# Two more rows of the attention weights turned by VectorE, one transfer group fewer for TensorE, and a shorter ring of rooms

## What is computed

```python
def _attention(q, k, v):
    logits = jnp.einsum('bqhd,bkhd->bhqk', q.astype(jnp.float32), k.astype(jnp.float32))
    logits = logits / jnp.sqrt(jnp.float32(q.shape[-1]))
    logits = jnp.where(mask, logits, neg)
    probs = jax.nn.softmax(logits, axis=-1).astype(dtype)
    return jnp.einsum('bhqk,bkhd->bqhd', probs, v)
...
xn = _layernorm(x, axis=-1)
x = x + _L0_attn_ref(xn, w_qkv, w_out) + _L0_ffn_ref(xn, wg, w1, b1, w2, b2)
```

## Time and profile before

| | |
|---|---|
| median of 3 runs | 2915.57 us (2914.02 to 2918.3) |
| the profiled execution, its own time | 2915.7 us |
| its span, first to last instruction | 2913.9 us |
| mean granted TensorE clock | 0.988 |
| PE busy | 2814.5 us (97%) |
| DVE busy | 2084.7 us (72%) |
| ACT busy | 1699.7 us (58%) |
| POOL busy | 1723.0 us (59%) |

### The profile page before, as it was taken

One profiled execution on the slowest core, in us unless ns is written; L12 is line 12 of the kernel. 1 busy time (PEld: TensorE's weight loads), 2 busy tenths in 40 slices (PEclk: granted clock), 3 DMA queues, 4 the chain that ended last, 5 costly groups with the idle time before them and its releaser, 6 DMA issues.

```text
span 2913.9 us, 61264 instructions
## 1 busy us (share of the span) xinstructions
PE 2814.5 (97%) x21321; PEld 2284.1 (78%) x21321; DVE 2084.7 (72%) x4448; ACT 1699.7 (58%) x3934; POOL 1723.0 (59%) x2631
## 2 busy tenths in 40 slices
PE   5599999999998999999999999999999999999998
PEld 4489999899997777777777777777777777777776
DVE  7843444344434888888888888888888888888886
ACT  3454444445454666666666666666666666666664
POOL 3032122211212777777877877777777778777774
PEclk9799999999999999999999999999999999999999
DMA  7022212221212565665665565665665556556553
GB/s 241 29 82 75 69 52 83 76 68 47 82 54 74 141 158 144 163 154 145 168 150 145 147 170 147 157 166 142 157 164 151 149 146 176 141 145 183 136 134 93
DMA packets 248774, 371.58 MB, mean 128 GB/s; under 512 B 77392, under 2 KB 177744, under 8 KB 248480
## 3 DMA queue, kind: packets, MB, share of 16 engines
q1 hardware_dynamic: 216000, 276.31, 35.3%
q0 software_dynamic: 32480, 91.44, 11.7%
HBM read 102.80 MB, written 33.55 MB: 47 GB/s over the span
## 4 chain that ended last, share of the span: by engine, by line
PE 66%; DVE 1%; SPq 1%; DMA 0%; issue 0%; ACT 0%; POOL 0%; DVEq 0%; ACTq 0%
PE O L1263 18%; PE S L1231 16%; PE W L1142 12%; PE W L1157 7%; PE W L1176 7%; PE W L1187 6%; SPq L1085 1%; DVE pr L1355 0%; PE W L1165 0%; DMA pT<-squares 0%; DVE squares L1398 0%; ACT pr L1293 0%; DMA out<-res 0%; ACT pT L1283 0%; DVE res L1381 0%
## 5 line engine op out<-in xcount | busy, mean ns | idle before, releaser
L1436 POOL TENSOR_SCALAR pr<-pr,rinv 128x512 f32<-128x512 f32 (+7 forms) x1024 | 748.4, 744 | 399.7 <-DVE rinv L1361 398.6
L1293 ACT ACTIVATE pr<-pr,negm 128x512 f32<-128x512 f32 (+7 forms) x1024 | 787.3, 774 | 285.3 <-DVE negm L1355 285.3
L1355 DVE CUSTOM_DVE_ANT_0 pr<-S,late 128x512 f32<-128x512 f32 (+7 forms) x1024 | 717.0, 751 | 112.9 <-PE S L1231 112.9
L1263 PE MATMUL O<-pT,vv 128*64 128x256 f32 (+1 forms) x5120 | 541.3, 362 | 3.1 <-DMA pT<-squares 3.1
L1398 DVE STREAM_TRANSPOSE squares<-pr 128x640 f32<-128x640 f32 x504 | 494.8, 1020 | 0.0
L1263 PEld LDWEIGHTS O<-pT,vv 128*64 128x64 f32 x5120 | 346.4, 137 | 181.8 <-issue 20.4
L832 DVE TENSOR_TENSOR hl<-h,hh 128x512 fp32r<-128x512 f32 x256 | 192.3, 751 | 315.2 <-ACT hh L793 315.0
L789 ACT ACTIVATE h<-pH,b1c 128x512 f32<-128x512 f32 x256 | 175.9, 687 | 366.0 <-PE pH L719 334.1
L1283 ACT ACTIVATE pT<-W 128x512 f32<-128x512 f32 (+3 forms) x520 | 199.6, 437 | 215.8 <-PE W L1187 215.8
L731 PE MATMUL pY<-w2h,hh 128*128 128x256 f32 x1024 | 287.7, 281 | 2.5 <-DVE hl L832 2.5
L731 PE MATMUL pY<-w2l,hh 128*128 128x256 f32 x1024 | 289.1, 282 | 0.0
(11 more groups left out here) (176 smaller groups left out, 6479.6 us busy)
## 6 DMA issues: line engine op xcount, KB each, us to landing
pT<-squares SPq DMA_DIRECT2D x756, 128.0 KB
pT<-squares SPq DMA_DIRECT2D x756, 96.0 KB, 2.8
pT<-squares POOLq DMA_DIRECT2D x252, 128.0 KB
pT<-squares POOLq DMA_DIRECT2D x252, 96.0 KB, 3.0
y<-yb SPq DMA_DIRECT2D x128, 128.0 KB, 1.7
wr<-in_L_attn_w_qkv SPq DMA_DIRECT2D x128, 128.0 KB, 2.3
x<-in_L_attn_x SPq DMA_DIRECT2D x16, 512.0 KB, 8.9
xn<-xn SPq DMA_DIRECT2D x16, 512.0 KB, 4.4
```

What stands on the lines that cost most here:

```text
L1263: ins = e.matmul(O[hs, o0 + a:o0 + GQ], vv[n // 2 % 2][:, kt, vs], turned_p, start=(kt == 0), stop=(kt == KT - 1))
L1293: e.activation(p, p, ACT.Exp, bias=negm[:, c0:c0 + 1], scale=-1.0, accum_out=rsum[:, c0:c0 + 1]).then_inc(expd.sem, 1)
L1355: e.tensor_tensor_reduce(room_of(n, i, h)[:, off:off + w], S[h][:, off:off + w], late[:, SEQ - w:], 1.0, -MASKED, ALU.add, ALU.min, negm[: ...
L1436: e.tensor_scalar(p, p, rinv[:, c0:c0 + 1], 1.0, ALU.mult, ALU.mult).then_inc(scaled.sem, 1)
```

## The change

Rows 3 and 2 are turned by DVE in squares as rows 4 to 7 are. Their squares lie next to those of rows 4 and 5 in one buffer (`squares12`), and one group of 16 transfers moves both groups 1 and 2 to `pT12`; a transfer of it is 32 x 1280 elements instead of 32 x 768. PE's pieces t30, t31, t20 and t21 and ACT's copies of them are gone. The rooms are two rounds instead of three. Row 1 and row 0 are still turned by PE, but one round earlier: t1 at step 8 instead of 13, t0 at step 12 instead of 16. Row 1 is scaled ahead of row 4. Run 0 stands at step 7 instead of 3 and run 1 at step 11 instead of 7. Several pieces move: v1 from step 4 to 2, p1 from 10 to 4, o0 and o1 to steps 9 and 10, o2 from 11 to 13. On DVE the low part of a projection and `xnl` stand ahead of the squares of their step. In the last unit only rows 6 and 7 are still turned by PE.

```diff
-    SUB, RING = 4, 3
+    SUB, RING = 4, 2
-    SCALE_ORDER = [(i, h) for rows in ROUNDS for i in (rows if 0 not in rows else rows[::-1]) for h in range(2)]
+    SCALE_ORDER = [(i, h) for rows in ROUNDS for i in (rows if 3 in rows else rows[::-1]) for h in range(2)]
...
-    SQUARED = [4, 5, 6, 7]
-    in_squares = lambda n, i: i in SQUARED and n < UNITS - 1
+    SQUARED = [(i, h) for i in (3, 2, 4, 5, 6, 7) for h in range(2)]
+    TURNED_LAST = (6, 7)
+    in_squares = lambda n, i: i > 1 and (n < UNITS - 1 or i not in TURNED_LAST)
...
-    ACT_STEP = {"v0": 2, "xn": 2, "v1": 6, "t30": 8, "t31": 8, "t20": 8, "t21": 9, "p1": 12,
-                "p0": 12, "t1": 13, "t0": 16, "p2": 17, "p3": 18}
-    DVE_STEP = {"xn": 3, "o0": 6, "o1": 10, "p1": 12, "o2": 12, "p0": 15, "p2": 19, "p3": 19, "o3": STEPS + 2}
+    ACT_STEP = {"v0": 2, "xn": 2, "v1": 4, "p1": 6, "t1": 8, "t0": 12, "p0": 13, "p2": 17, "p3": 18}
+    DVE_STEP = {"xn": 2, "p1": 6, "o0": 10, "o1": 10, "p0": 14, "o2": 15, "p2": 18, "p3": 19, "o3": STEPS}
...
-    RUN_STEP = [(1, 3), (1, 7), (1, 15)]
+    RUN_STEP = [(1, 7), (1, 11), (1, 15)]
...
-                e.wait_ge(squared.sem, squared.at(n, 4 * g - 4))
+                e.wait_ge(squared.sem, squared.at(n, 4 * g))
...
-                if x == 2 and 0 <= m < UNITS and in_squares(m, ROUNDS[q][0]):
-                    for h in range(2):
-                        square(m, ROUNDS[q][0], h)
+                if x == 2 and 0 <= m < UNITS:
+                    for i in ROUNDS[q]:
+                        if in_squares(m, i):
+                            for h in range(2):
+                                square(m, i, h)
```

More of the change, by code:

```diff
@@ L874, in attention_and_sum @@
     column = lambda n, i, h: 4 * room(n, i) + 2 * ROUNDS[ROUND_OF[i]].index(i) + h
-    SQUARED = [4, 5, 6, 7]
-    in_squares = lambda n, i: i in SQUARED and n < UNITS - 1
-    TURNS = {"t30": [(3, 0, 0, 4)], "t31": [(3, 1, 0, 4)], "t20": [(2, 0, 0, 3)], "t21": [(2, 1, 0, 3)],
-             "t1": [(1, 0, 0, 2), (1, 1, 0, 2)], "t0": [(0, 0, 0, 1), (0, 1, 0, 1)]}
-    TURNS |= {f"t{i}{h}{c}": [(i, h, c * HT, min(HT, i + 1 - c * HT))] for i in SQUARED for c in range(-(-(i + 1) // HT)) for h in range(2)}
@@ new lines, in attention_and_sum @@
+    TURNS = {"t1": [(1, 0, 0, 2), (1, 1, 0, 2)], "t0": [(0, 0, 0, 1), (0, 1, 0, 1)]}
+    TURNS |= {f"t{i}{h}{c}": [(i, h, c * HT, min(HT, i + 1 - c * HT))] for i in TURNED_LAST for c in range(-(-(i + 1) // HT)) for h in range(2)}
+    STEP_OF = {"v0": 0, "xn": 1, "v1": 2,
+               "p1": 4,
+               "t1": 8, "o0": 9, "o1": 10,
+               "t0": 12, "p0": 12, "o2": 13,
+               "p2": 16, "p3": 17, "o3": 18}
+    ACT_STEP = {"v0": 2, "xn": 2, "v1": 4, "p1": 6, "t1": 8, "t0": 12, "p0": 13, "p2": 17, "p3": 18}
@@ L899, in attention_and_sum @@
+    DVE_STEP = {"xn": 2, "p1": 6, "o0": 10, "o1": 10, "p0": 14, "o2": 15, "p2": 18, "p3": 19, "o3": STEPS}
+    BANK_OF = {"v0": 0, "xn": 2, "v1": 1,
+               "p1": 2,
+               "t1": 2, "o0": 1, "o1": 0,
+               "t0": 2, "p0": 1, "o2": 0,
+               "p2": 0, "p3": 1, "o3": 2}
+    END_STEP = {6: (UNITS, 0), 7: (UNITS, 4)}
     DVE_STEP |= {f"t6{h}{c}": 2 for h in range(2) for c in range(2)}
@@ L953, in attention_and_sum @@
         vv = two(lambda i: sb(f"vv{i}", [P, QT, VW]))
-        pT = [sb(f"pT{g}", [P, 2, 2 * g + 2, GQ]) for g in range(GROUPS)]
-        sq = {g: sb(f"squares{g}", [P, QUARTERS, 4, 2 * g + 2, BL]) for g in (2, 3)}
-        wide = {g: pT[g][:].rearrange("p h k q -> p (h k q)").rearrange("p (a x r) -> p a x r", x=4, a=QUARTERS) for g in (2, 3)}
+        BLOCK = {g: 4 * (2 * g + 2) * BL for g in (1, 2, 3)}
+        pT0, pT3 = (sb(f"pT{g}", [P, 2, 2 * g + 2, GQ]) for g in (0, 3))
+        pT12, sq12 = (sb(n, [P, QUARTERS, BLOCK[1] + BLOCK[2]]) for n in ("pT12", "squares12"))
+        sq3 = sb("squares3", [P, QUARTERS, BLOCK[3]])
+        pT = {0: pT0[:], 3: pT3[:]}
+        wide = {1: pT12[:, :, :BLOCK[1]], 2: pT12[:, :, BLOCK[1]:],
+                3: pT3[:].rearrange("p h k q -> p (h k q)").rearrange("p (a r) -> p a r", a=QUARTERS)}
+        wide = {g: w.rearrange("p a (x r) -> p a x r", x=4) for g, w in wide.items()}
+        sq = {1: sq12[:, :, :BLOCK[1]], 2: sq12[:, :, BLOCK[1]:], 3: sq3[:]}
+        sq = {g: w.rearrange("p b (x k i) -> p b x k i", x=4, i=BL) for g, w in sq.items()}
+        whole = {2: (pT12[:], sq12[:]), 3: (wide[3].rearrange("p a x r -> p a (x r)"), sq3[:])}
         pr = start.pr + [sb(f"pr{i}", [P, SEQ]) for i in range(len(start.pr), 2 * RING)]
@@ L1026, in _ @@
             def _(e):
-                for g in (2, 3):
+                for g in (1, 2, 3):
                     e.memset(sq[g][:, :, 0::2, 2 * g + 1, :], 0.0)
@@ L1032, in attention_and_sum @@
         recip = Count(sem("s_recip"), len(ROUNDS))
-        squared = Count(sem("s_squared"), 2 * len(SQUARED))
+        squared = Count(sem("s_squared"), len(SQUARED))
         placed = {2: Count(sem("s_placed2"), 16 * QUARTERS * (QUARTERS - 1)), 3: Count(sem("s_placed3"), 16 * QUARTERS * (QUARTERS - 1))}
@@ L1066, in strip @@
             to, of = slice(b * BL, (b + 1) * BL), slice(a * BL, (a + 1) * BL)
-            return wide[g][to, a].rearrange("p x r -> p (x r)"), sq[g][of, b].rearrange("p x k i -> p (x k i)")
+            placed_in, squares = whole[g]
+            return placed_in[to, a], squares[of, b]
         @block.sync
@@ L1117, in _ @@
                         refill(b, g)
-                if n < UNITS - 1:
-                    place(n, 2)
+                place(n, 2)
                 if n % 2 == 0 and n // 2 + 2 < UNITS // 2:
@@ L1237, in values @@
                 groups = RUN_GROUPS[j]
[L1238 to L1247, removed]
+                for g in groups:
+                    if in_squares(n, 2 * g):
+                        e.wait_ge(placed[max(g, 2)].sem, placed[max(g, 2)].at(n + 1, 0))
+                        e.wait_ge(pool_placed[max(g, 2)].sem, pool_placed[max(g, 2)].at(n + 1, 0))
+                    else:
+                        for m, name in [(turn_unit(n, t), t) for i in (2 * g, 2 * g + 1) for t in turns_of(i)]:
+                            if by_act(name):
+                                e.wait_ge(act.sem, act.at(m, name))
+                            else:
+                                e.wait_ge(dve.sem, dve.at(m, name))
                 if j == 0:
@@ L1348, in row_min @@
                             if in_squares(m, of):
-                                e.wait_ge(squared.sem, squared.at(m, 2 * SQUARED.index(of) + h + 1))
+                                e.wait_ge(squared.sem, squared.at(m, SQUARED.index((of, h)) + 1))
                             else:
@@ L1393, in square @@
                 g, KT = i // 2, i + 1
-                if n > 0 and i % 2 == 0 and h == 0:
-                    e.wait_ge(placed[g].sem, placed[g].at(n, 0))
-                    e.wait_ge(pool_placed[g].sem, pool_placed[g].at(n, 0))
+                if n > 0 and i in (3, 6) and h == 0:
+                    e.wait_ge(placed[max(g, 2)].sem, placed[max(g, 2)].at(n, 0))
+                    e.wait_ge(pool_placed[max(g, 2)].sem, pool_placed[max(g, 2)].at(n, 0))
                 e.wait_ge(scaled.sem, scaled.at(n, SCALE_ORDER.index((i, h)) + 1))
@@ L1518, in _ @@
                         place_rest(n - 1, 3)
-                    elif name == "place2" and n < UNITS - 1:
+                    elif name == "place2":
                         place_rest(n, 2)
```

## The result

The changed kernel takes 3130.45 us (median of 4 runs; one of them, 3422.56 at a mean granted clock of 0.748 where the others had 0.965 or 0.966, is left out of the ratio). Measured beside it, the kernel before took 2914.8 us. The ratio is 1.0738, with a 95% interval of 1.0717 to 1.0759: 7.4% slower. The prediction was 3130 us, in a range of 3045 to 3190. The profiled execution took 3129.8 us, with a span of 3128.0, 214.1 more than before.

A forecast was written before the change was run, and what follows sets the result against it. A loop through PE, DVE and POOL was to bound the unit at 33.35 us, 2.54 above before: 2915.7 + 160 = 3076 us, plus 54 for the clock = 3130. Range 3045 to 3190, 80 in 100.

The forecast's parts named there:

- The loop: Once per unit through PE, DVE and POOL: 13.63 + 6.85 + 11.48 + 1.19 + 0.20 hand-overs = 33.35 us.
- The waits for ACT: DVE waits for ACT's copies in each unit: 0.70 us ahead of `ql`, 0.82 of `xnl`, 0.91 of `klf`.
- One way out of the list: From r1's reciprocals on DVE, the loop was followed only through POOL's scaling of row 1 (1.19 us) to t1.
- Where PE waits: PE idles 4.36 us per unit: some 3.3 at t1, the rest ahead of S1 and S2.
- The clock: PE's waits lower its clock, 1.7 us per unit: nothing to 107 us in all, the middle, 54, taken.
- Two rounds of rooms at nothing: Row minima waiting for turns two rounds back cost nothing; t1 and t0 are over before r3 and r4 begin.
- The larger transfers at nothing: SP's 12 issues take 7.54 us, leaving some 6 us for the last to land before run 0; no cost.
- The last units: In the last unit 22 fewer transposes and a later run 0 about cancel, within 3 us.
- PE without gaps: Rival: row 1 is scaled before PE reaches t1; unit 28.99 us, kernel 2801; 6 in 100.
- DVE's waits for ACT: Rival: the three waits, 2.43 us together, vanish; loop 30.92 us, kernel 2923; 6 in 100.
- The squares do not hold POOL: Rival judged: new squares on DVE delay POOL's row 1 by up to 2.18 us; kernel 3267; 5 in 100.
- transfers set the unit: Sign of a wrong forecast: PE's waits at the runs for transfers; no size or chance given.

The follow-up runs named there:

- run 0: Not a follow-up run: a piece of products on PE in each unit, which needs SP's transfers of groups 1 and 2; no time or ratio of its own.
- e2: Changed kernel with the low parts `xnl`, `klf` and both `ql` put back behind the squares of their step on DVE: 2965.17 us, ratio 1.0172.
- e1: Changed kernel with t1 moved from step 8 to 12 and t0 from 12 to 14 on PE: 3120.29 us, ratio 1.0696.
- e6: Changed kernel with the four new squares on DVE behind r1's reciprocals but ahead of `ol`: 3122.56 us, ratio 1.0721.
- e3: Changed kernel with 16 added identity transposes on PE ahead of t1's wait in each unit: 3092.44 us, ratio 1.0607.
- e7: Kernel before the change with two rounds of rooms instead of three, two last-unit turns two steps earlier: 2965.99 us, ratio 1.0179.
- e12: e11 with SP's refills at batch starts each put ahead of what needs it: 2892.77 us, ratio 0.9908 to the kernel before.
- e11: Changed kernel with e1's and e2's edits, SP's batch-start stores and refills split, and run 0 ahead of p1 on PE: 2932.01 us, ratio 1.0048.

## Why the prediction was right, point by point

- **The loop.** Right in all four parts, 33.40 measured for 33.35. The waits for ACT were 0.65, 0.78 and 0.86 (predicted 0.70, 0.82, 0.91), the squares 2027.96 - 2025.82 = 2.14 (2.18). That the loop is closed by the order of DVE's list is shown by e2, which changes only places on DVE and takes 2.19 us off the unit.
- **One way out of the list.** Too simple. I followed only POOL and t1. e1 shows o0 behind `ol` at nearly the same length, and e6 POOL's own list. For the time of the changed kernel the longest counts, and that was the one I added up.
- **Where PE waits.** Roughly right: at t1 2.5 and 2.6 in the two units shown, for 3.3. The rest was put ahead of S1 and S2 without sizes: S1 waits 0.42, S2 not at all; p1 waits 0.66 for POOL's `wl` and xn 0.45 for its bank, and neither was foreseen. The four make some 4.1 for 4.36.
- **The clock.** The middle of the bounds, 54 us, was a choice; 38 is what e3 gets back. Of the 48 ordinary units 28 pay some 1.4 each (48 x (34.22 - 33.39) / 28), and 20 nothing.
- **Two rounds of rooms at nothing.** No wait speaks against it in this kernel; without the squares it is wrong (e7).
- **The larger transfers at nothing.** Right in ordinary units, where run 0 hardly ever waits, but closer than it says: some 6 us were left for the last transfer to land, and it lands 1.2 ahead of run 0 (median). Wrong in the seven first units of the batches. I had worked out SP's 12 issues and not what stands ahead of them at a batch start. Those units are 36.54 - 34.22 = 2.32 longer than the others, 16 us in all, where before they were 0.36 longer.
- **The last units.** Taken like the others (loop and clock, 3.40 more each), the last eight are only 1.21 longer: they have no xn piece, so no `xnl` and no wait for it. The end behind the last minimum is 5.5 longer, where I said within 3. Two parts show on PE:

```profile
3103.76 3.68 PE L1194 MATMUL W<-ident,pr 128*128 128x128 f32 x16 [0.65 <-DVE pT L1290]
3109.18 2.38 PE L1270 MATMUL O<-pT,vv 128*64 128x256 f32 x24 [1.75 <-issue]
```

  The turns of row 7 run at a granted clock of 0.50 (from 3101 to 3107), 0.23 us each for 0.13, and run 0 then waits 1.75 us, until 0.20 after its last transfer has landed. The remainder is left open.

Of the 214 us, the middle of the forecast had 160 from the loop and 54 from the clock. Measured, the loop gives some 148 (2.51 in each of 55 units and 9.7 in the last eight), the clock 40, the batch starts some 20 beyond the loop, and the two ends 7. The first two are 26 less than forecast, the last two 27 more. So the mechanism and the range were earned, and meeting 3130 within 1 us was luck.

- **The rivals.** PE without gaps never came, not even in e12 (30.2 per unit for PE's own 28.99). DVE's waits for ACT did not vanish by themselves, but e2 takes them away: 31.20 for the 30.92 that this rival had, and 2965 for 2923, of which the batch starts (7 x (35.34 - 31.24) = 29) are the larger part. The squares do not hold POOL (e6). That transfers set the unit is true only of the seven first units here, and in part of e11 and e12.

## What to carry to other kernels

When work moves from the busiest engine to one with idle time, look at what stands behind it in that engine's list: here 2.1 us of squares and 2.3 us of waits for copies were in front of a reciprocal for which three other engines waited, directly or through each other. Taking one way out of such a list away only shows the next: e1 gave 0.3%, and e6 no more than its noise. What stands in the list ahead of all ways out is worth moving first: e2, which takes the waits away, gave 5.3% alone, and 6.5% with e1. And a list of transfers has its own rare places: what comes once per eight units must be read there, not in an ordinary unit.

## What was not expected of the hardware

More work made the kernel faster: 16 transposes in each unit that compute nothing for the result gave 38 us back, as the stretches at a granted clock of 0.51 disappeared from the ordinary units. With waits of 2.51 and 2.59 us at t1 in two units that follow each other, only the second was followed by such a stretch; what decides it the runs do not tell.
